# Third attention: scores as three F32R products, keys kept as high and low parts and replaced in place

## The chip, the cores and the metric

The program runs on one core of one Trainium2 chip, as one launch. The metric is the device time of an execution in microseconds; lower is better. Five engines work side by side, each with a queue of its own: TensorE (PE, with its weight loads as PEld), VectorE (DVE), ScalarE (ACT), GpSimd (POOL) and SyncE (SP), which here issues the DMAs. They wait for one another by semaphores.

## The reference

The input is x (64 batches of 128 rows of 128 numbers) and a context of 64 x 77 x 96. Eight layers follow one another, each adding to x: attention 0 (16 heads, masked), a SiLU layer, attention 1 (8 heads), a quantised layer, attention 2 (16 heads, this case), a gated mixture of experts, a wide attention and a routed mixture. Attention 2, which the text calls the third attention, computes

```
q = (x @ Wq).reshape(b, n, h, d).transpose(0, 2, 1, 3)      # h = 16 heads, d = 64; x is normalised first
k = (context @ Wk).reshape(b, -1, h, d).transpose(0, 2, 1, 3)
v = (context @ Wv).reshape(b, -1, h, d).transpose(0, 2, 1, 3)
sim = jnp.einsum('bhid,bhjd->bhij', q, k) * scale
attn = jax.nn.softmax(sim, axis=-1)
out = jnp.einsum('bhij,bhjd->bhid', attn, v)
return out.transpose(0, 2, 1, 3).reshape(b, n, h * d) @ Wo + bo
```

## The kernel before

Weights are folded first: with Wq Wk^T per head (mt) the scores are z times "keys", where keys = mt^T times the context (128 x 77 per head and batch) and z is the normalised x, turned; with Wv Wo per head (vo) the output is a sum over heads of probabilities times "values" (77 x 128 per head and batch). Projections of keys and values are made as three F32R products of high and low parts (`three_passes`, lines 84 to 89): high x high, low x high, high x low. The scores and the weighted sum are plain F32 matmuls.

The class `CrossAttention` is one program for three attentions. The batches run in order, t = 0 to 63; four make a group, eight a window (i = 0 to 7 within it, k = i mod 4). One batch has 16 x 77 = 1232 score columns in three PSUM banks (6, 6 and 4 heads: 462, 462 and 308 columns). `window` in `tensor` (974 to 1013) does for batch t: transposes of the probabilities of t (`turn_chunks`, ten blocks in three uses of ps_t), then the scores of batch t+2 (`scores`, line 891), at k = 1 the turning of the next group's z, then the weighted sum of batch t (`weighted_sum`, line 904). Between these, `project_next` sets projections, in the order of a plan written out by hand (lines 613, 614): keys of the next group, `key_plan` (4,3,2,5,4,5,2,7), and values of the next window, `val_plan` (3,4,4,2,3,2,2,0). One key projection is one head for four batches (308 columns), one value projection 128 or 104 rows by 512 columns; they use the two banks ps_p in turn. 32 keys and 20 values a window.

The keys stand in two buffers, one per group parity (line 650). ScalarE copies key projections there (`copy_keys`, 1022), value projections into one of five staging slots (`copy_values`, 1031), from which SyncE stores two projections at a time to HBM (`store_values`, 822); `load_values` (835, 837) fetches each batch's values two batches ahead. ScalarE also copies the transposed probabilities (1059, 1062) and z (1049), and takes the exponentials (1067) in the order of `window` in `scalar`: copies of t's transposes, then the exponentials of t+1, then the remaining projections' copies.

VectorE's order per batch (`body`, 1266): at k = 1 z of the next group (236); `normalise` of batch t+1 (reduce 1197, reciprocal 1199, multiply 1205); `shift` of batch t+2 (maxima 1153, subtractions 1189 from PSUM into the buffer e, two of which alternate); the residual of batch t (1221); statistics (190, 195, 290, 292). The subtractions free the score banks; the exponentials wait for them. GpSimd has small work: per group the bias (225), two powers (209, 304) and their sums, per window two copies that reorder the context (`copy_window`, 1390), for which it waits until the window's last probabilities are done (1342). Ahead of the loop stands a start-up: 20 values, 16 + 7 keys, z, the scores of batches 0 and 1.

## Time and profile before

| what | us |
|---|---|
| median of three runs | 2406.95 (2406.39 to 2409.49) |
| the profiled execution | 2405.5 |
| its span, first to last instruction | 2403.6 |
| TensorE busy | 2222.6 (92%) |
| VectorE busy | 1857.5 (77%) |
| ScalarE busy | 1492.9 (62%) |
| GpSimd busy | 685.1 (29%) |
| granted TensorE clock, mean | 0.961 of full speed |

The page's 40 slices are 60 us each. TensorE's digits are 9 nearly everywhere; the third attention fills slices 21 to 30 (about 1240 to 1840 us), where GpSimd's digit is mostly 1. A timeline row gives start, duration, engine, line, operation, written tile and read tiles, and "x3" means three merged instructions. Durations overlap on an engine, since instructions are pipelined; the pace is the distance of starts. A plain F32 matmul shows as two records.

### The profile page before, as it was taken

The numbers are of one execution on the slowest core, as the hardware profiler recorded it, in microseconds if no ns is written. First come the engines' busy times: TensorE is split into PE (matmuls) and PEld (weight loads), VectorE is DVE, ScalarE is ACT, GpSimd is POOL, SyncE is SP. The second block draws the span as 40 slices with busy tenths as digits, with TensorE's granted clock in tenths as the row PEclk, the third lists the DMA queues.
The fourth block names the chain that finished last, engine by engine and source line by source line (L and its number), as shares of the span: only waits on it lengthen the run. The fifth ranks groups of instructions, "written<-read, shape, count | busy, mean of one in ns | idle before, by whom it ended". The sixth has DMA issues, their size and how long they took to land.

```text
span 2403.6 us, 49297 instructions
## 1 busy us (share of the span) xinstructions
PE 2222.6 (92%) x14668; PEld 1910.2 (79%) x14669; DVE 1857.5 (77%) x4483; ACT 1492.9 (62%) x3090; POOL 685.1 (29%) x926
## 2 busy tenths in 40 slices
PE   7899999999899899995478999999997999979999
PEld 6688888888698788872257888888886888879998
DVE  3688888888976888887975887887888666866666
ACT  5566666665445677767886666666664654636666
POOL 2255546555412122210001111111102442422334
PEclk9999999999999999997589999999998999979999
DMA  8444554445201444430025445454442000114545
GB/s 216 114 137 129 145 144 138 134 140 151 68 0 47 114 133 126 137 111 15 0 72 146 132 134 153 137 145 140 140 132 62 1 1 3 37 53 139 141 140 158
DMA packets 461646, 256.58 MB, mean 107 GB/s; under 512 B 25664, under 2 KB 442332, under 8 KB 461532
## 3 DMA queue, kind: packets, MB, share of 16 engines
q1 hardware_dynamic: 461532, 255.27, 37.7%
q8 instruction: 46, 0.75, 0.1%
q14 instruction: 68, 0.56, 0.1%
HBM read 150.10 MB, written 105.12 MB: 106 GB/s over the span
## 4 chain that ended last, share of the span: by engine, by line
PE 75%; DVE 12%; ACT 6%; issue 5%; POOL 0%; ACTq 0%; DVEq 0%; POOLq 0%
PE ps_o L904 13%; PE ps_s L891 11%; PE ps_p L87 7%; PE ps_p L89 6%; PE ps_p L88 6%; PE ps_t L881 6%; PE ps_o L1474 3%; PE ps_t L1474 2%; PE ps_t L3129 2%; PE ps_s L3111 2%; PE ps_o L3129 2%; PE ps_s L87 2%; ACT a_keys L1022 2%; DVE a_sm L1197 2%; PE ps_s L89 2%
## 5 line engine op out<-in xcount | busy, mean ns | idle before, releaser
L904 PEld LDWEIGHTS ps_o<-a_val,a_pt 128*128 128x128 f32 (+2 forms) x3200 | 413.6, 192 | 35.0 <-issue 8.4
L904 PE MATMUL ps_o<-a_val,a_pt 128*128 128x128 f32 (+2 forms) x3200 | 423.9, 276 | 5.7 <-ACT a_pt L1059 3.6
L891 PE MATMUL ps_s<-a_keys,a_zt 128*128 128x308 f32 (+1 forms) x1024 | 415.7, 492 | 14.6 <-ACT a_keys L1022 9.8
L1031 ACT ACTIVATE a_stage<-ps_p 128x512 f32<-128x512 f32 (+1 forms) x370 | 221.1, 598 | 276.9 <-PE ps_p L89 275.0
L1197 DVE TENSOR_REDUCE a_sm<-a_e 128x16 f32<-128x1232 f32 (+1 forms) x192 | 234.2, 1220 | 183.2 <-ACT a_e L1067 182.7
L1059 ACT ACTIVATE a_pt<-ps_t 128x512 f32<-128x512 f32 (+1 forms) x448 | 225.2, 505 | 151.1 <-PE ps_t L881 149.8
L1022 ACT ACTIVATE a_keys<-ps_p 128x308 f32<-128x308 f32 x603 | 256.7, 427 | 81.8 <-PE ps_p L89 81.4
L881 PE MATMUL ps_t<-ident,a_e 128*128 128x128 f32 (+1 forms) x1600 | 262.8, 277 | 32.9 <-POOL a_e L1214 16.4
L87 PE MATMUL ps_p<-ct_hi,a_mt_hi 96*128 (+1 forms) x603 | 293.0, 486 | 0.0
L1067 ACT ACTIVATE a_e<-a_e 128x1232 f32<-128x1232 f32 (+1 forms) x192 | 203.9, 1062 | 50.9 <-DVE a_e L1189 34.6
L1214 POOL TENSOR_TENSOR a_e<-a_e,a_rs 128x539 f32<-128x539 f32 (+1 forms) x192 | 165.6, 890 | 234.6 <-DVE a_rs L1202 233.2
L881 PEld LDWEIGHTS ps_t<-ident,a_e 128*128 128x128 f32 (+1 forms) x1600 | 194.1, 140 | 44.0 <-issue 19.0
L87 PE MATMUL ps_p<-a_vo_hi,a_windowhi 96*128 96x512 f32 (+1 forms) x370 | 207.9, 562 | 5.2 <-ACT a_keys L1022 3.9
L891 PEld LDWEIGHTS ps_s<-a_keys,a_zt 128*128 128x128 f32 x1024 | 169.5, 191 | 41.5 <-issue 22.5
L89 PE MATMUL ps_p<-ct_hi,a_mt_lo 96*128 (+1 forms) x603 | 184.3, 306 | 0.0
L88 PE MATMUL ps_p<-ct_lo,a_mt_hi 96*128 (+1 forms) x603 | 184.0, 305 | 0.0
L1153 DVE TENSOR_REDUCE a_mx<-ps_s 128x6 f32<-128x462 f32 (+1 forms) x320 | 155.9, 533 | 27.2 <-PE ps_s L891 26.9
L225 POOL TENSOR_TENSOR x<-x,a_bias 128x512 f32<-128x512 f32 (+1 forms) x48 | 61.3, 1276 | 340.9 <-DVE z L353 203.4
L1189 DVE TENSOR_TENSOR a_e<-ps_s,a_mx 128x462 f32<-128x462 f32 (+1 forms) x320 | 154.3, 532 | 0.0
L1205 DVE TENSOR_TENSOR a_e<-a_e,a_rs 128x616 f32<-128x616 f32 (+1 forms) x128 | 146.2, 1142 | 4.4
L88 PEld LDWEIGHTS ps_p<-ct_lo,a_mt_hi 96*128 96x128 f32 x603 | 116.4, 193 | 39.0 <-issue 32.1
L89 PE MATMUL ps_p<-a_vo_hi,a_windowlo 96*128 96x512 f32 (+1 forms) x370 | 146.3, 395 | 0.0
(437 smaller groups left out, 4931.6 us busy)
## 6 DMA issues: line engine op xcount, KB each, us to landing
a_vals<-a_stage SPq DMA_DIRECT2D x160, 512.0 KB, 3.5
a_val<-a_vals SPq DMA_DIRECT2D x128, 576.0 KB
f_w<-in_L_ffn_W_dram SPq DMA_DIRECT2D x129, 256.0 KB, 2.7
a_vals<-a_stage SPq DMA_DIRECT2D x40, 416.0 KB
a_val<-a_vals SPq DMA_DIRECT2D x64, 256.0 KB
a_val<-a_vals SPq DMA_DIRECT2D x128, 40.0 KB
x<-in_x_dram SPq DMA_DIRECT2D x8, 512.0 KB, 7.0
out_dram<-x SPq DMA_DIRECT2D x7, 512.0 KB, 6.8
```

The costliest lines, as they stand in the source:

```text
L87: eng.matmul(out, lhs[0], rhs[0], start=start, stop=False)
L88: eng.matmul(out, lhs[0], rhs[1], start=False, stop=False)
L89: return eng.matmul(out, lhs[1], rhs[0], start=False, stop=stop)
L881: mm = eng.transpose(c.ps_t[0:w, slot, (i % GT) * P:(i % GT + 1) * P], src[:, P * i:P * i + w], c.ident[:, :])
L891: eng.matmul(c.ps_s[:, b, 0:nh * KEYS], zt, keys[:, h0:h0 + nh, :], start=True, stop=True)\
L904: mm = eng.matmul(c.ps_o[:, (i % 2) * P:(i % 2 + 1) * P], self.pt[0:r, n, :], self.val[0:r, i % 2, n, :], start=(n == 0), stop=(n == self. ...
L1022: eng.activation(self.keys[:, par, :, h, :], bank[:, 0:GCOLS].rearrange("p (b k) -> p b k", b=GT), ACT.Copy)\
L1031: eng.activation(self.stage[0:n, slot, BANK * (v % 2):BANK * (v % 2) + BANK], bank[0:n, :], ACT.Copy)\
L1059: mm = eng.activation(dst[:, i0:full, :], src[:, 0:full - i0, :], ACT.Copy)
L1067: eng.activation(self.e[:, par, :], self.e[:, par, :], ACT.Exp).then_inc(self.exp_ready.sem, 1)
L1197: eng.tensor_reduce(self.sm[:, :], e, AX.X, ALU.add).then_inc(st.sem, 1)
L1214: eng.tensor_tensor(e[:, heads, :], e[:, heads, :], bc(self.rs[:, par, heads], KEYS), ALU.mult)\
```

## The change

Only the third attention changes (`split=name == "L2"`).

- z and keys are held as F32R high and low parts. `scores` issues `three_passes` for each of the three banks, instead of one F32 matmul.
- z: ScalarE's copy now writes the high part; VectorE writes the low part (`split_zt`, one subtraction of 128x512 from PSUM), at k = 1 after `shift`.
- There is one keys buffer (a high and a low one) in place of two. `freed_by` gives for each scored batch the four heads of the next group that its space takes; the layout alternates between group parities (`unit_of`, `batch_of`). The plan has four keys a batch; each stands on TensorE after the scores that free its space: one behind the third bank, one behind the first and second part of the weighted sum, the last at its end. Values go 3,3,3,3,3,3,2,0, ahead of them.
- ScalarE copies a key projection into a ring of four slots (`keep_keys`), waiting until GpSimd has split what was there. GpSimd makes both parts (`split_keys`: a cast and a dependent subtraction of 128x308) and no longer waits for probabilities ahead of `copy_window`. At k = 2, TensorE waits before each bank of scores for the last split that this bank reads.
- Staging slots go from five to two; the first window's values also use e and pt for staging, so VectorE's first `shift` and ScalarE's loop wait for those stores.
- Start-up: 20 values and 16 keys, whose low parts VectorE writes (`split_first_keys`), then z and its low part, scores of batches 0 and 1, and only then eight keys of the next group, copied by ScalarE around its first exponentials and split by GpSimd. The next layer's weight split on GpSimd comes after them.

```diff
+        self.split, self.in_place = split, split and H == 16
+        self.slots = 2 if self.in_place else self.STAGES
+        self.first_rounds = self.units // self.STAGES
+        self.rounds = self.units // self.slots
         self.key_plan = (4, 3, 2, 5, 4, 5, 2, 7) if H == 16 else (2, 2, 1, 2, 2, 2, 2, 3)
         self.val_plan = (3, 4, 4, 2, 3, 2, 2, 0) if H == 16 else (2, 1, 2, 1, 2, 2, 0, 0)
+        if self.in_place:
+            self.val_plan = (3, 3, 3, 3, 3, 3, 2, 0)
...
-        self.first = self.vuses + H + self.key_plan[-1]
+        self.early_keys = 2 * self.quads if self.in_place else 0
+        self.lead = self.vuses + H + (0 if self.in_place else self.key_plan[-1])
+        self.first = self.lead + self.early_keys
...
-        self.keys = sb(ctx, n("keys"), [P, 2, GT, H, KEYS], F32)
+        if split:
+            self.keys_hi, self.keys_lo = (sb(ctx, n("keys" + h), [P, 1 if self.in_place else 2, GT * H, KEYS], F32R)
+                                          for h in ("hi", "lo"))
+            self.zt_lo = sb(ctx, n("ztlo"), [P, 2, GT * P], F32R)
+            self.unsplit = sb(ctx, n("unsplit"), [P, self.RING, GT, KEYS], F32)
+        else:
+            self.keys = sb(ctx, n("keys"), [P, 2, GT, H, KEYS], F32)
...
-        self.stage = sb(self.stage_scope, n("stage"), [P, self.STAGES, self.PART * P], F32)
+        self.stage = sb(self.stage_scope, n("stage"), [P, self.slots, self.PART * P], F32)
...
+    def freed_by(self, k, par):
+
+        q = self.quads
+        return [2 * k, 2 * k + 1, 2 * k + 8, 2 * k + 9] if par == 0 else [q * k + j for j in range(q)]
+
+    def make_plan_in_place(self, last):
+
+        plan, place, v = [], 0, 0
+        for i in range(self.WIN):
+            mine = []
+            if not last:
+                for _ in range(self.val_plan[i]):
+                    mine.append(("v", v, place))
+                    v, place = v + 1, place + 1
+            if not last or i < 2:
+                for h in self.freed_by((i + 2) % GT, self.key_group(i) % 2):
+                    mine.append(("k", h, place))
+                    place += 1
+            plan.append(mine)
...
+    def batch_of(self, keys, par, k, b):
+
+        h0, nh = self.head_span(b)
+        if not self.in_place:
+            return keys[:, par].rearrange("p (k h) c -> p k h c", k=GT)[:, k, h0:h0 + nh, :]
+        if par == 0:
+            return keys[:, 0].rearrange("p (k h) c -> p k h c", k=GT)[:, k, h0:h0 + nh, :]
+        pairs = keys[:, 0].rearrange("p (m k h) c -> p m k (h c)", k=GT, h=2)
+        return pairs[:, h0 // 2:(h0 + nh) // 2, k, :]
...
+    def stage_of(self, w, u):
+
+        if not self.in_place or not (isinstance(w, int) and w == 0):
+            return u % self.slots, u // self.slots, self.stage[:, u % self.slots, :]
+        slot, width = u % self.STAGES, self.PART * P
+        places = [self.stage[:, 0, :], self.stage[:, 1, :], self.e[:, 0, 0:width], self.e[:, 1, 0:width],
+                  self.pt[:, 0:width // P, :].rearrange("p i d -> p (i d)")]
+        return slot, u // self.STAGES, places[slot]
...
-    def scores(self, eng, t, b, zt, keys, first=False):
+    def scores(self, eng, t, b, par, k, first=False):
 
         c = self.core
         h0, nh = self.head_span(b)
         if not first:
             eng.wait_ge(self.scores_read.sem, self.scores_read.at(self.NB * (t - 1) + b + 1))
-        eng.matmul(c.ps_s[:, b, 0:nh * KEYS], zt, keys[:, h0:h0 + nh, :], start=True, stop=True)\
-           .then_inc(self.scores_ready.sem, 1)
+        o, cols = c.ps_s[:, b, 0:nh * KEYS], slice(k * P, k * P + P)
+        if self.split:
+            mm = three_passes(eng, o, [z[:, par, cols] for z in (self.zt_hi, self.zt_lo)],
+                              [self.batch_of(keys, par, k, b) for keys in (self.keys_hi, self.keys_lo)])
+        else:
+            mm = eng.matmul(o, self.zt[:, par, cols], self.keys[:, par, k, h0:h0 + nh, :], start=True, stop=True)
+        mm.then_inc(self.scores_ready.sem, 1)
...
+                if self.split and u - 5 >= self.vuses:
+                    eng.wait_ge(self.key_split.sem, self.key_split.at(u - 5 - self.vuses + 1))
...
+        for n in range(self.early_keys):
+            u = self.lead + n
+            if n >= 2:
+                eng.wait_ge(self.proj_copied.sem, self.proj_copied.at(u - 1))
+            self.project_keys(eng, c.ps_p[:, n % 2, :], 1, self.freed_by(n // self.quads, 1)[n % self.quads])
...
+                        if k == 2 and self.split:
+                            eng.wait_ge(self.key_split.sem,
+                                        self.key_split.at(self.keys_for(w, par, b, last) + 1))
+                        elif k == 2:
                             eng.wait_ge(self.proj_copied.sem,
                                         self.proj_copied.at(self.keys_use(w, par, b, last) + 1))
-                        self.scores(eng, t + 2, b, self.zt[:, par2, n2 * P:(n2 + 1) * P], self.keys[:, par2, n2])
-                        project_next()
+                        self.scores(eng, t + 2, b, par2, n2)
+                        project_next(scored=b == self.NB - 1)
...
+                    project_next(self.WIN if j == self.uses - 1 else 1, scored=True)
...
+    def keep_keys(self, eng, u, bank, n, slot):
+
+        eng.wait_ge(self.key_split.sem, self.key_split.at(n - self.RING + 1))
+        eng.wait_ge(self.proj_done.sem, self.proj_done.at(u + 1))
+        eng.activation(self.unsplit[:, slot, :, :], bank[:, 0:GCOLS].rearrange("p (b k) -> p b k", b=GT), ACT.Copy)\
+           .then_inc(self.proj_copied.sem, 1)
...
+        slot, turn, place = self.stage_of(w, unit)
         if v % 2 == 0 and not (isinstance(w, int) and w == 0 and turn == 0):
-            eng.wait_ge(self.stored[slot].sem, self.stored[slot].at(16 * (self.rounds * w + turn)))
+            eng.wait_ge(self.stored[slot].sem, self.stored[slot].at(self.stored_by(w, turn)))
...
+        for n in range(min(2, self.early_keys)):
+            self.keep_keys(eng, self.lead + n, c.ps_p[:, n % 2, :], self.heads + n, (self.heads + n) % self.RING)
         self.exponentials(eng, 0, 0)
+        for n in range(2, self.early_keys):
+            self.keep_keys(eng, self.lead + n, c.ps_p[:, n % 2, :], self.heads + n, (self.heads + n) % self.RING)
+        if self.in_place:
+            eng.wait_ge(self.stored[4].sem, self.stored[4].at(16 * self.first_rounds))
...
+    def split_first_keys(self, eng):
+
+        for u in range(self.vuses, self.lead):
+            g, h = (u - self.vuses) // self.heads, (u - self.vuses) % self.heads
+            eng.wait_ge(self.proj_copied.sem, self.proj_copied.at(u + 1))
+            bank = self.core.bank(u % 5)[:, 0:GCOLS].rearrange("p (b k) -> p b k", b=GT)
+            eng.tensor_tensor(self.unit_of(self.keys_lo, g % 2, h), bank,
+                              self.unit_of(self.keys_hi, g % 2, h).bitcast(F32), ALU.subtract)\
+               .then_inc(self.key_split.sem, 1)
+
+    def split_zt(self, eng, g, par, u, slot):
+
+        eng.wait_ge(self.t_copied.sem, self.t_copied.at(u + 1))
+        eng.tensor_tensor(self.zt_lo[:, par, :], self.core.ps_t[:, slot, :],
+                          self.zt_hi[:, par, :].bitcast(F32), ALU.subtract).then_inc(self.zt_split.sem, 1)
...
+                if self.split and k == 1 and not last:
+                    u = 1 + self.gcyc * g + 2 * self.uses
+                    self.split_zt(eng, g + 1, 1 - par, u, (1 + self.gcyc * par + 2 * self.uses) % 2)
...
-        if self.next_stats and not self.setup:
+        if self.next_stats and not self.setup and not self.split:
             self.after.split_weights(eng)
         v_last = max(place for mine in self.plan for kind, _, place in mine if kind == "v")
...
+    def split_keys(self, eng, u, n, par, h):
+
+        src = self.unsplit[:, n % self.RING, :, :]
+        hi, lo = self.unit_of(self.keys_hi, par, h), self.unit_of(self.keys_lo, par, h)
+        eng.wait_ge(self.proj_copied.sem, self.proj_copied.at(u + 1))
+        eng.tensor_copy(hi, src).then_inc(self.key_high.sem, 1)
+        eng.wait_ge(self.key_high.sem, self.key_high.at(n - (self.lead - self.vuses) + 1))
+        eng.tensor_tensor(lo, src, hi.bitcast(F32), ALU.subtract).then_inc(self.key_split.sem, 1)
+
+    def gpsimd_split(self, eng, v_last):
+
+        for n in range(self.early_keys):
+            self.split_keys(eng, self.lead + n, self.lead - self.vuses + n, 1,
+                            self.freed_by(n // self.quads, 1)[n % self.quads])
+        self.ln.pool(eng, 1)
+        if self.next_stats:
+            self.after.split_weights(eng)
+
+        def window(w, more, last):
+            for i in range(self.WIN):
+                for kind, h, place in self.plan_of(i, last):
+                    if kind == "k":
+                        self.split_keys(eng, self.use(w, place), self.key_number(w, place, last),
+                                        self.key_group(i) % 2, h)
+                g = 2 * w + 1 + i // GT
+                if last and i >= GT:
+                    break
+                if i % GT == 2:
+                    self.ln.pool_bias(eng, g)
+                    if self.left and g >= 3:
+                        self.left.root(eng, g - 3)
+                    if self.next_stats and g >= 2:
+                        self.next_stats.pool(eng, g - 2)
+                    if more and i >= GT:
+                        eng.wait_ge(self.proj_done.sem, self.proj_done.at(self.use(w, v_last) + 1))
+                        self.copy_window(eng, w + 2)
+                elif i % GT == 3 and g + 1 < GROUPS:
+                    self.ln.pool(eng, g + 1)
...
+            banks_free=(ahead.added, GROUPS - 1) if name == "L1" else None, split=name == "L2")
```

## Rows read from the trace of the kernel before

**Rows 1.** Stretch, length, busy us (instructions) by engine, clock, DMA share, GB/s

```profile
1410.83:1482.48 71.65, 71.65 (x454) 61.30 (x452) 57.82 (x121) 44.74 (x95) 9.79 (x13) 1.00 0.49 141
```

**Rows 2.** Chain of waits in the third attention: start us, us, what

```profile
1410.24 0.78 PE ps_s L891 x2
1411.45 0.52 PE ps_s L891 x2
...
1416.45 0.44 PE ps_t L881 x4
...
1421.87 2.23 PE ps_o L904 x20
```

**Rows 3.** Timeline of TensorE at that attention's first projections: start us, us, instruction

```profile
1264.87 0.39 PE L89 MATMUL ps_p<-a_vo_hi,a_windowlo 96*104 96x512 f32 x1
1265.10 0.30 PE L87 MATMUL ps_s<-ct_hi,a_mt_hi 96*128 96x308 f32 x1
1265.24 0.31 PE L88 MATMUL ps_s<-ct_lo,a_mt_hi 96*128 96x308 f32 x1
```

**Rows 4.** Timeline of VectorE and ScalarE over one batch, idle time before in brackets

```profile
1410.83 1.44 DVE L1197 TENSOR_REDUCE a_sm<-a_e 128x16 f32<-128x1232 f32 x1 [1.34 <-ACT a_e L1067]
...
1412.59 1.44 DVE L1205 TENSOR_TENSOR a_e<-a_e,a_rs 128x1232 f32<-128x1232 f32 x1
...
1413.94 1.56 DVE L1153 TENSOR_REDUCE a_mx<-ps_s 128x6 f32<-128x462 f32 x3
...
1415.42 1.56 DVE L1189 TENSOR_TENSOR a_e<-ps_s,a_mx 128x462 f32<-128x462 f32 x3
...
1418.90 1.24 ACT L1067 ACTIVATE a_e<-a_e 128x1232 f32<-128x1232 f32 x1
...
1420.17 1.44 DVE L1197 TENSOR_REDUCE a_sm<-a_e 128x16 f32<-128x1232 f32 x1 [2.58 <-ACT a_e L1067]
```

**Rows 5.** Timeline of VectorE in the last window

```profile
1802.24 1.43 DVE L1197 TENSOR_REDUCE a_sm<-a_e 128x16 f32<-128x1232 f32 x1
...
1809.71 1.44 DVE L1197 TENSOR_REDUCE a_sm<-a_e 128x16 f32<-128x1232 f32 x1 [0.16 <-ACT a_e L1067]
```

**Rows 6.** GpSimd's groups by shape, whole run: busy us, mean ns | idle before

```profile
L1214 POOL TENSOR_TENSOR a_e<-a_e,a_rs 128x539 f32<-128x539 f32 x128 | 136.7, 1089 | 234.6 <-DVE a_rs L1202 233.2
...
L1214 POOL TENSOR_TENSOR a_e<-a_e,a_rs 128x154 f32<-128x154 f32 x64 | 31.5, 492 | 0.0
...
L1390 POOL CAST a_windowlo<-ct_lo 96x616 fp32r x5 | 6.4, 1285 | 0.0
...
L2313 POOL TENSOR_TENSOR f_w1lo<-f_w,f_w1hi 128x576 fp32r<-128x576 f32 x1 | 1.4, 1442 | 0.1
...
L2311 POOL CAST f_w1hi<-f_w 128x576 fp32r<-128x576 f32 x1 | 0.7, 682 | 0.0
...
L2616 POOL TENSOR_TENSOR a_wklo<-a_wk,a_wkhi 96x128 fp32r<-96x128 f32 x1 | 0.5, 453 | 0.1
...
L2615 POOL CAST a_wkhi<-a_wk 96x128 fp32r<-96x128 f32 x1 | 0.3, 286 | 0.1
```

**Rows 7.** Durations of two VectorE lines, ns min/median/max

```profile
L1205 DVE TENSOR_TENSOR a_e<-a_e,a_rs x59: 799/800/1149, 800.8 to 1079.4; 128x616 f32<-128x616 f32 x59
...
L3222 DVE TENSOR_SCALAR f_z<-x,tail_mean_var,tail_rstd x64: 333/339/1325, 2138.4 to 2375.0; 128x128 f32 x48, 128x128 f32<-128x128 f32 x16
```

**Rows 8.** Timeline of GpSimd and VectorE where both work

```profile
152.88 1.67 POOL L1390 CAST a_windowlo<-ct_lo 96x616 fp32r<-96x616 f32 x1
...
877.17 1.28 POOL L225 TENSOR_TENSOR x<-x,a_bias 128x512 f32 x1 [9.68 <-DVE z L353]
...
877.96 1.15 DVE L1205 TENSOR_TENSOR a_e<-a_e,a_rs 128x616 f32<-128x616 f32 x1
```

**Rows 9.** Stores of values (line 822), from 1300 to 1800 us

```profile
DMA to landing us min/median/max: 3.2/3.5/5.2
```

**Rows 10.** Timeline of TensorE at that attention's first transposes, idle in brackets

```profile
1287.16 1.11 PE L881 MATMUL ps_t<-ident,a_e 128*128 128x128 f32 x4 [5.27 <-DVE a_e L1205]
```

More of the change, by code:

```diff
@@ L588 @@
     BLOCKS = -(-KEYS // KBLOCK)
+    RING = 4
     STAGES = 5
@@ L1094, in scalar @@
         eng.wait_ge(self.prod_done.sem, self.prod_done.at(self.pairs))
-        for u in range(self.first):
+        for u in range(self.lead):
             if u < self.vuses:
```

130 lines of the change are left out of this document (100 added, 30 removed).

## The prediction

> **What bounds the kernel now.** I read the page's slices first, then one window of eight batches of the third attention, then its chain of waits, then each engine's timeline inside it. That attention runs from about 1240 to 1840 us; its loop repeats windows of 71.65 us, in which TensorE is busy all 71.65, VectorE 57.82, ScalarE 44.74 and GpSimd 9.79 [rows 1]. TensorE bounds it, at full granted clock. The reader should see in the chain that a score bank of 462 columns costs 0.78 us, one of 308 0.52, four transposes 0.44, the ten blocks of the weighted sum 2.23 [rows 2]. F32R passes follow each other after 0.23 us at 512 columns (1264.87 to 1265.10) and after 0.14 at 308 [rows 3], so a value projection is 3 x 0.23 = 0.69 and a key projection 0.42. Ten transposes are 2.5 times four, 1.10; turning z is four more. Check: 8 x (1.10 transposes + 2.08 scores + 2.23 sum) + 32 keys x 0.42 + 20 values x 0.69 + 2 x 0.44 for z = 71.4, against 71.65.
>
> Behind TensorE stands a ring: exponentials, VectorE's normalise (reduce, reciprocal, multiply: 3.11 from 1410.83 to 1413.94), maxima 1.48, subtractions 1.48, then exponentials again 1.24 [rows 4]. It needs about 7.4 us a batch, and in the last window, where TensorE has almost nothing to project, batches follow at 7.47 [rows 5]. On average TensorE takes 8.96, so the ring has about 1.5 us to spare; the multiply of 1412.59 ends at 1414.03 and TensorE wants it at 1416.45 [rows 2, 4].
>
> **The change part by part.** *Scores.* A pass of 462 columns lies between 0.14 and 0.23; by interpolation 0.21, so 0.62 for three against 0.78; the small bank takes 0.42 against 0.52. Saved: 2 x 0.16 + 0.10 = 0.42 us a batch, 3.4 a window. Ends: if the pass costs what 512 columns do, 0.28 a batch; at 0.20, 0.46.
>
> *Plan.* Values go 3,3,3,3,3,3,2,0 and keys four a batch, the same 20 and 32 in all. TensorE's batches become 4.99 (1.10 + 1.66 + 2.23) + 1.68 keys + 2.07 values = 8.74, 9.18 where z is turned, 8.05 in batch 6, and 6.67 in batch 7. Batch 7 is then shorter than the ring's 7.47, with some wait on a port (below) 7.7: 1.0 lost a window. Before, seven keys stood there (4.99 + 0.42 + 7 x 0.42 = 8.35).
>
> *z in two parts.* VectorE adds one PSUM-SBUF subtraction of 512 columns every four batches, some 0.55 us; it comes after the subtractions, where the next normalise waits for the exponentials anyway (idle 2.58 us before 1420.17 in [rows 4]). Costs nothing in the loop; 0.55 at the start.
>
> *Keys in two parts.* ScalarE's copy is the same size, now into a ring of four slots. GpSimd gets a cast and a subtraction of 128x308 per head, four a batch. The rows nearest: the cast is 0.286 at 128 columns and 0.682 at 576, by interpolation 0.445 at 308; the subtraction 0.453 and 1.442, so 0.85 [rows 6]. With about 0.07 between the dependent pair: 1.36 us a head. Lower end: the attention's own GpSimd multiply, 1.089 at 539 and 0.492 at 154 columns, gives 0.73 at 308, with the cast 1.2. Upper end: if writing chunks of 77 hurts a cast as the window copy's scattered reads hurt it (1.285 at 616 columns, so 0.64) and the subtraction rises alike to 1.05, 1.75. I take 1.36 because the form of those rows (F32R out, two full F32 inputs) is the same. Per window: 32 x 1.36 = 43.5, plus the 9.8 of today = 53.3.
>
> *The port.* VectorE's multiply of probabilities in the second attention takes 0.80 alone, and 1.15 where GpSimd's addition of 877.17 was still running as it began: it ended 0.66 after that addition. In the other direction GpSimd's cast of 152.88 took 1.67 for 1.285, beside a VectorE operation on two SBUF inputs. VectorE's scaling of z takes 0.339, and up to 1.325 beside GpSimd's work [rows 6 to 8]. So multiply and GpSimd exclude each other, and each waits for the other's running instruction; reductions and operations that read PSUM show no such stretch. The Trainium skill has this as a rule ("SBUF — State Buffer", section "SBUF: two separate sides"): an operation with two SBUF inputs and a GpSimd operation hold a shared pair of ports whole; the trace agrees. A multiply of 1.44 a batch blocks GpSimd up to 11.5 a window, eight z operations of 0.26 another 2.1. GpSimd's window: 53.3 + 13.6 = 66.9, of TensorE's 68.25 plus losses. It fits, barely, but not evenly. VectorE in turn waits some 0.3 for GpSimd before a multiply; its slack of over 1 us covers that in batches with three values, not in batch 7 (the 7.7 above).
>
> *The new wait.* The scores of batches 2 and 6 read a new group of keys, so TensorE waits for GpSimd's last splits; everything in TensorE's queue (scores, values, sums) stands behind that, and VectorE's maxima wait for it. From the last key projection to the third bank of the next batch are 1.10 + 3 x 0.69 + 2 x 0.62 = 4.4 us. After a quiet stretch GpSimd gets the first of four keys 5.7 us into the batch, is held by the multiply to about 7.5 and ends the fourth 3.2 to 3.7 into the next batch: in time by 0.7 or more. After batch 6 it is not quiet: bias and statistics (2.6) and the window copies (2.5) come on top, no longer held back by their wait for the probabilities. Followed on, GpSimd ends the keys of batch 7 about 9.1 us into batch 0, those of batch 0 9.2 into batch 1, those of batch 1 5.3 into batch 2: 0.9 late, once a window. With 1.43 a head it is 2.3.
>
> *Stores.* Two staging slots instead of five: ScalarE waits for a store two units back, issued at least 8.3 us earlier; stores land in 3.2 to 5.2 us [rows 9]. Nothing, with 3 us to spare; if that cover went, ScalarE and both projection banks would stand.
>
> *Start.* Seven keys fewer ahead of the first scores, 7 x 0.42 = 2.9 gained; 0.55 for z's low part; 0.35 for GpSimd's early splits meeting the first multiplies: 2.0 gained. The eight early keys go into the 5.27 us in which TensorE waits for probabilities today [rows 10]. Shift's wait for the stores from the e buffer: they had landed by then. Last window: ring-bound before and after, 0.
>
> Sum: a window 71.65 - 3.4 + 1.0 + 0.9 = 70.15, 1.5 gained, seven times 10.5, and 2.0 at the start: 12.5 us. The profiled execution took 2405.5 (span 2403.6), so 2393.0; the median of the three runs is 1.45 above it, 2406.95, so **2394.5**.
>
> **The rivals.** *GpSimd short by a little* (1.43 to 1.5 a head): 2.3 or more late a window, gain 0.1 or less: 2401 to 2407, take 2405. For it: 66.9 of 68 is no margin. Against: interpolated prices. Chance 0.16.
>
> *GpSimd becomes the bound.* Place: the splits, 32 heads a window. At p us a head its window is 32p + 9.8 + 13.6, with some 1.5 of idling; it passes 71.65 from p = 1.46 on if every lock falls due, from 1.55 if some don't, and the wait shows as TensorE standing in batches 2 and 6 and ScalarE standing at its ring. At 1.6: 76.1, less the locks that don't fall due (about 3): 73, slower by 1.5 x 7 - 2 = 8.5: 2415; at 1.75: 78, 2449. For: chunks of 77, no row has that shape. Chance 0.20, at 2416.
>
> *The port matters little.* If multiplies and splits seldom meet, GpSimd has 53.3 of work and is never late: 71.65 - 3.4 + 0.9 = 69.15, so 7 x 2.5 + 2 = 19.5: 2387.5. With batch 7 not losing either: 2381. Against: the first split arrives at 5.8, the multiply at 6.0, in nearly each batch. Chance 0.18.
>
> *The passes are no faster*, because each needs its own weight load and that sets the pace: 1.0 + 0.9 lost a window, 7 x 1.9 - 2 = 11.3: 2418. Against: at 308 columns passes with a load each follow in 0.14 [rows 3]. Chance 0.04.
>
> **How the numbers follow.** Forecast 0.42 (2388 to 2400), the others as above. No change means within 0.2%, about what a measurement of this kernel can tell: 2402 to 2412. Faster: 0.42 + 0.18 + 0.03 = 0.63. Within: 0.13 of the first rival and 0.02 of the second = 0.15. Slower: 0.22. The range reaches from the rival at 2382 to the bound at 2418, leaving 0.07 below and 0.12 above.
>
> **What would show it.** Right: score banks in the chain at 0.62 and 0.42; windows near 70.2; GpSimd busy 52 to 55 a window with casts near 0.45 and subtractions near 0.85 unless a multiply lies on them; multiplies stretched from 1.44 to 1.6 to 1.9; batch 7 at 7.7; a TensorE wait for GpSimd's key parts of about 1 us in batch 2. Wrong: subtractions above 1 us, TensorE waiting for key parts in each group, ScalarE waiting for the ring or a store, or the ring of softmax pacing all batches.

## The result, and the profile after

The changed kernel is slower: 2421.56 us (2419.98 to 2427.11) against 2409.49 (2406.39 to 2411.1) for the kernel before on the same chip, a ratio of 1.0057 with a 95% interval of 1.0046 to 1.0069. The forecast was 2394.5 and faster. The profiled execution took 2421.56 us, its span 2419.8; the one before took 2405.5 and 2403.6.

The first look is at the same stretch as [rows 1]: eight batches of the third attention, from one normalise (L1345, first operation on VectorE) to the ninth. Columns: stretch, length, busy us (instructions) of TensorE, its weight loads, VectorE, ScalarE and GpSimd, granted clock, DMA share, GB/s.

```profile
1416.24:1489.69 73.45, 69.95 (x478) 64.02 (x477) 60.29 (x122) 46.84 (x95) 56.46 (x76) 1.00 0.48 137
```

The window has grown from 71.65 to 73.45 us. TensorE has less to do (69.95 for 71.65) and for the first time it waits. Seven windows of 1.8 us are 12.6 of the 15.8 us by which the attention, from its first value projection to its last residual, is longer (593.4 before, 609.3 after). The steps that shorten TensorE's work are there: this is TensorE's timeline, the passes of one score bank of 462 columns.

```profile
1278.05 0.38 PE L88 MATMUL ps_s<-a_keyslo,a_zthi 128*128 128x462 f32 x1
1278.26 0.37 PE L89 MATMUL ps_s<-a_keyshi,a_ztlo 128*128 128x462 f32 x1
1278.47 0.37 PE L87 MATMUL ps_s<-a_keyshi,a_zthi 128*128 128x462 f32 x1
```

They follow each other after 0.21 us, so three are 0.63 where one F32 product was 0.78 [rows 2]. What took the gain back is in TensorE's waits over the whole run (us in total, times, longest):

```profile
PE ps_t L985 <- DVE a_ztlo L1385: 14.2, 15, 2.1
PE ps_p L87 <- POOL a_windowlo L1614: 8.4, 6, 1.4
```

Neither is the wait that the prediction had costed (scores for GpSimd's key parts); that one doesn't occur in the whole run. The first, in the timelines of VectorE, ScalarE and TensorE:

```profile
1454.54 1.44 DVE L1353 TENSOR_TENSOR a_e<-a_e,a_rs 128x1232 f32<-128x1232 f32 x1
1455.90 1.56 DVE L1301 TENSOR_REDUCE a_mx<-ps_s 128x6 f32<-128x462 f32 x3
1457.38 1.56 DVE L1337 TENSOR_TENSOR a_e<-ps_s,a_mx 128x462 f32<-128x462 f32 x3
1458.86 0.68 DVE L1385 TENSOR_TENSOR a_ztlo<-ps_t,a_zthi 128x512 fp32r<-128x512 f32 x1
```
```profile
1454.19 0.60 ACT L1187 ACTIVATE a_zthi<-ps_t 128x512 fp32r<-128x512 f32 x1
```
```profile
1457.52 0.60 PE L985 MATMUL ps_t<-ident,a_e 128*128 128x128 f32 x4
...
1459.67 0.54 PE L985 MATMUL ps_t<-ident,a_e 128*128 128x128 f32 x3 [0.85 <-DVE a_ztlo L1385]
```

Turned z lies in one of the two slots of `ps_t`. ScalarE has written its high part by 1454.79, but VectorE reads the slot again for the low part, only after the maxima and subtractions, at 1458.86. The second transposes of the next batch need that slot and stand until 1459.67. It happens once a group, twice a window.

The second, in the timelines of GpSimd and TensorE:

```profile
1433.60 1.28 POOL L225 TENSOR_TENSOR x<-x,a_bias 128x512 f32<-128x512 f32 x1
1434.85 0.19 POOL L297 TENSOR_TENSOR tail_var<-tail_mean_var,eps 128x4 f32<-128x4 f32 x1
1435.12 1.02 POOL L304 TENSOR_TENSOR tail_rstd<-tail_var,neg_half 128x4 f32<-128x4 f32 x1
1436.20 2.34 POOL L1614 CAST a_windowhi<-ct_hi 96x616 fp32r<-96x616 f32 x1
1438.50 1.22 POOL L1614 CAST a_windowlo<-ct_lo 96x616 fp32r<-96x616 f32 x1
```
```profile
1439.77 0.50 PE L87 MATMUL ps_p<-a_vo_hi,a_windowhi 96*128 96x512 f32 x1 [1.41 <-POOL a_windowlo L1614]
```

The context of the next window is copied by GpSimd behind eight splits, the bias and the statistics, and batch 0 of that window projects its first value from it: 1.41 us, once a window. Batches are counted from 0 to 7 here, as in the prediction.

### The profile page after: what moved, and what is told of

It reads as the page before. It is cut to its first block, busy times and chain, and to the rows that moved or that the text cites. A ratio compares the mean times of both kernels' runs of the same rounds, so it can differ in the third digit from the quotient of the medians.

```text
span 2419.8 us, 50496 instructions
## 1 busy us (share of the span) xinstructions
PE 2211.7 (91%) x14860; PEld 1934.1 (80%) x14861; DVE 1886.0 (78%) x4515; ACT 1509.5 (62%) x3090; POOL 1033.6 (43%) x1406
## 4 chain that ended last, share of the span: by engine, by line
PE 66%; DVE 16%; ACT 7%; issue 5%; POOL 3%; ACTq 0%; DVEq 0%; POOLq 0%
PE ps_o L1013 10%; PE ps_p L87 6%; PE ps_s L1000 6%; PE ps_p L89 5%; PE ps_p L88 5%; PE ps_t L985 5%; PE ps_o L1698 3%; DVE a_sm L1345 3%; PE ps_s L87 3%; PE ps_t L1698 2%; PE ps_t L3353 2%; PE ps_s L89 2%; PE ps_s L88 2%; PE ps_o L3353 2%; PE ps_s L3335 2%
## 5 line engine op out<-in xcount | busy, mean ns | idle before, releaser
L1013 PE MATMUL ps_o<-a_val,a_pt 128*128 128x128 f32 (+2 forms) x3200 | 429.3, 276 | 5.7 <-ACT a_pt L1197 3.6
L1345 DVE TENSOR_REDUCE a_sm<-a_e 128x16 f32<-128x1232 f32 (+1 forms) x192 | 234.2, 1220 | 179.1 <-ACT a_e L1205 178.8
L87 PE MATMUL ps_p<-ct_hi,a_mt_hi 96*128 (+1 forms) x608 | 264.7, 435 | 2.3 <-ACT a_unsplit L1149 2.2
L1000 PE MATMUL ps_s<-a_keys,a_zt 128*128 128x308 f32 (+1 forms) x640 | 252.9, 481 | 12.8 <-ACT a_keys L1158 9.8
L1568 POOL TENSOR_TENSOR a_keyslo<-a_unsplit,a_keyshi 128x308 fp32r<-128x308 f32 x240 | 229.4, 956 | 19.2
L87 PE MATMUL ps_p<-a_vo_hi,a_windowhi 96*128 96x512 f32 (+1 forms) x370 | 191.4, 517 | 13.7 <-POOL a_windowlo L1614 8.4
L1149 ACT ACTIVATE a_unsplit<-ps_p 128x308 f32<-128x308 f32 x240 | 102.5, 427 | 162.2 <-PE ps_p L89 158.8
L1158 ACT ACTIVATE a_keys<-ps_p 128x308 f32<-128x308 f32 x362 | 153.8, 427 | 43.7 <-PE ps_p L89 43.3
L1566 POOL CAST a_keyshi<-a_unsplit 128x308 fp32r<-128x308 f32 x240 | 123.4, 514 | 113.8 <-ACT a_unsplit L1149 113.2
```

The source lines that it names most:

```text
L87: eng.matmul(out, lhs[0], rhs[0], start=start, stop=False)
L1000: mm = eng.matmul(o, self.zt[:, par, cols], self.keys[:, par, k, h0:h0 + nh, :], start=True, stop=True)
L1013: mm = eng.matmul(c.ps_o[:, (i % 2) * P:(i % 2 + 1) * P], self.pt[0:r, n, :], self.val[0:r, i % 2, n, :], start=(n == 0), stop=(n == self. ...
L1345: eng.tensor_reduce(self.sm[:, :], e, AX.X, ALU.add).then_inc(st.sem, 1)
L1568: eng.tensor_tensor(lo, src, hi.bitcast(F32), ALU.subtract).then_inc(self.key_split.sem, 1)
```

## The experiments

Theory A: these two waits alone turn the prediction's gain into a loss, and the rest of its sum holds. Rival B: the round of VectorE and ScalarE (the prediction's ring: exponentials, normalise, maxima, subtractions), or GpSimd, or the port it shares with VectorE, is the true limit, and the waits are where it happens to show. Ratios below are to the kernel before, run on the same chip; a percentage between two changed kernels is the difference of their ratios.

### Each wait alone, and both

```diff
-                if not (last and k >= 2):
-                    self.shift(eng, t + 2, k % 2, found)
                 if self.split and k == 1 and not last:
                     u = 1 + self.gcyc * g + 2 * self.uses
                     self.split_zt(eng, g + 1, 1 - par, u, (1 + self.gcyc * par + 2 * self.uses) % 2)
+                if not (last and k >= 2):
+                    self.shift(eng, t + 2, k % 2, found)
```

> The changed kernel with one step moved on VectorE: in the second batch of a group it forms the low part of the turned z right after the multiply, ahead of the maxima and subtractions of the batch after next. Theory A (TensorE's second transposes of every third batch wait 0.85 us for that low part, 12.1 us in 14 places, and nothing else is late there): those waits go, the window of eight batches falls from 73.45 to about 71.7 us, and the kernel by about 12 us, from 2421.6 to about 2409.5. Rival B (the round of VectorE and ScalarE, made longer by the stretched multiplies, is as late as TensorE; the wait is only where it shows): the subtractions come 0.7 us later, TensorE waits for the probabilities instead, and the kernel stays within 3 us of 2421.6.

Measured: ratio 0.9993 (0.9983 to 1.0003), 0.64% under the changed kernel, 15 us. The window is 71.26, 2.19 less; 7 x 2.19 = 15.3. In VectorE's timeline of this kernel the low part now stands straight behind the multiply, ahead of the maxima, and TensorE's second transposes start without a wait.

```profile
1449.70 1.44 DVE L1353 TENSOR_TENSOR a_e<-a_e,a_rs 128x1232 f32<-128x1232 f32 x1
1451.06 0.68 DVE L1385 TENSOR_TENSOR a_ztlo<-ps_t,a_zthi 128x512 fp32r<-128x512 f32 x1
1451.66 0.63 DVE L1301 TENSOR_REDUCE a_mx<-ps_s 128x6 f32<-128x462 f32 x1
```

The wait cost 1.1 us each time, not the 0.85 printed: the end of a TensorE record is modelled and reaches into the idle time. The window copy:

```diff
             for i in range(self.WIN):
+                if more and i == 6:
+                    eng.wait_ge(self.proj_done.sem, self.proj_done.at(self.use(w, v_last) + 1))
+                    self.copy_window(eng, w + 2)
                 for kind, h, place in self.plan_of(i, last):
...
-                    if more and i >= GT:
-                        eng.wait_ge(self.proj_done.sem, self.proj_done.at(self.use(w, v_last) + 1))
-                        self.copy_window(eng, w + 2)
```

> The changed kernel with one step moved on GpSimd: the copy of the next window's context (two casts, 4.1 us at the mean) stands ahead of the seventh batch's key splits instead of behind them, the bias and the statistics; GpSimd had 3.50 us idle there. Theory A (TensorE's first value projection of a window waits 1.41 us for that copy, six times): that wait goes, the window falls by about 1.4 us, the kernel by about 8.5 us to about 2413. Rival B (the key splits, now up to 1 us later, fill the ring of four, and ScalarE and then TensorE wait for them in batches 7 and 8 instead): the window stays within 0.5 us, the kernel within 3 us of 2421.6.

Measured: ratio 1.0026 (1.0014 to 1.0038), 0.31% or 7.5 us under the changed kernel. The window is 71.84, 1.61 less; six times that is 9.7, a little more than the kernel's time shows. Both moves together:

> Both moves together (low part of z ahead of the maxima on VectorE; window copy ahead of the seventh batch's splits on GpSimd). Theory A (TensorE is the bound and these two waits are all that the change added to its queue in a window): window 73.45 - 1.7 - 1.4 = about 70.35 us, near TensorE's busy 69.95; kernel 2421.6 - 12 - 8.5 = about 2401, faster than the kernel before (2409.5) by about 0.35%. Rival B (another engine holds the round at about 72 us): the two gains don't add, and the kernel stays above 2408.

Measured: 2395.09 us (2392.28 to 2397.07), ratio 0.9951 (0.9937 to 0.9965), which is 1.06% or 25 us under the changed kernel. The stretches of the three, one from each:

```profile
1429.38:1500.64 71.26, 69.47 (x478) 64.09 (x477) 60.27 (x122) 46.64 (x94) 56.45 (x77) 1.00 0.50 142
```
```profile
1436.22:1508.06 71.84, 69.74 (x478) 64.01 (x477) 60.03 (x122) 46.80 (x94) 56.59 (x77) 1.00 0.49 141
```
```profile
1427.34:1497.07 69.73, 69.30 (x478) 64.17 (x477) 60.05 (x122) 46.58 (x94) 56.53 (x77) 1.00 0.51 145
```

The gains add: 2.19 + 1.61 = 3.80, against 73.45 - 69.73 = 3.72, and in the kernel 7 x 2.19 + 6 x 1.61 = 25.0. VectorE, ScalarE and GpSimd are as busy as ahead of the moves. Rival B falls for these two waits.

### The start

```diff
+        self.exponentials(eng, 0, 0)
         for n in range(min(2, self.early_keys)):
             self.keep_keys(eng, self.lead + n, c.ps_p[:, n % 2, :], self.heads + n, (self.heads + n) % self.RING)
-        self.exponentials(eng, 0, 0)
```

> As the one with both moves, and ScalarE takes the first batch's exponentials ahead of the two early key copies. Theory: the first multiply comes 1.9 us earlier (the exponentials then start when VectorE's first subtractions end, 1281.8 for 1285.6), and the kernel is about 2 us under the one with both moves, about 2399. Rival: the second batch's exponentials stand behind the same key copies and GpSimd's ring anyway, so that the first batches end where they did and nothing is gained.

Measured: 2389.93 us (2388.01 to 2393.41), ratio 0.9938 (0.9925 to 0.9952), 0.13% or 3 us under the one without this edit, inside the intervals of the two. The first two normalises, of the changed kernel and of this one (VectorE's timelines):

```profile
1286.84 1.44 DVE L1345 TENSOR_REDUCE a_sm<-a_e 128x16 f32<-128x1232 f32 x1 [1.84 <-ACT a_e L1205]
1296.99 1.44 DVE L1345 TENSOR_REDUCE a_sm<-a_e 128x16 f32<-128x1232 f32 x1 [6.82 <-ACT a_e L1205]
```
```profile
1281.40 1.43 DVE L1345 TENSOR_REDUCE a_sm<-a_e 128x16 f32<-128x1232 f32 x1
1290.47 1.44 DVE L1345 TENSOR_REDUCE a_sm<-a_e 128x16 f32<-128x1232 f32 x1 [5.84 <-ACT a_e L1205]
```

Counted from the attention's first value projection (1252.91 and 1249.36), the first comes at 33.93 and 32.04 us, the second at 44.08 and 41.11. VectorE no longer stands 1.84 for the exponentials, as expected. Part of the difference at the second is clock, as the stretch from 1288 to 1300 shows (the changed kernel, then this one; the clock is the figure after GpSimd's, and this one had 1.00 over the ten us before too): a mean of 0.72 is time at both levels, 1.2 and 2.4 GHz, 1.00 all at 2.4.

```profile
1288.00:1300.00 12.00, 12.00 (x60) 10.35 (x59) 5.04 (x6) 6.85 (x14) 11.38 (x16) 0.72 0.15 45
```
```profile
1288.00:1300.00 12.00, 12.00 (x81) 11.09 (x79) 9.23 (x15) 8.86 (x19) 11.22 (x18) 1.00 0.48 141
```

With all three edits the attention takes 579.5 us, 13.9 less than in the kernel before (593.4), and 7 x (71.65 - 69.69) = 13.7 of that are the windows.

### What the terms of the sum are worth

The next three start from the kernel with all three edits (window 69.69 us, its row below). First its scores as one F32 product of the high parts:

```diff
-            mm = three_passes(eng, o, [z[:, par, cols] for z in (self.zt_hi, self.zt_lo)],
-                              [self.batch_of(keys, par, k, b) for keys in (self.keys_hi, self.keys_lo)])
+            mm = eng.matmul(o, self.zt_hi[:, par, cols].bitcast(F32),
+                            self.batch_of(self.keys_hi, par, k, b).bitcast(F32), start=True, stop=True)
```

> The kernel with both moves and the early exponentials, with the scores as one F32 product of the high parts: it leaves out the low parts, all splits are still made. This puts back the scores' price of the kernel before (0.78 + 0.78 + 0.52 = 2.08 us a batch for 1.68) and nothing else. Theory A: 8 x 0.42 = 3.4 us more a window, 69.7 -> 73.1, the kernel about 25 us slower, 2415. Rival (the gain of the three passes is partly lost at their seams, a pass after another kind of product starting late): under 2.5 more a window, under 18 us.

Measured: 2416.03 us, ratio 1.0029 (1.0017 to 1.0042), 0.91% or 22 us above the kernel with three passes; 7 x 3.03 = 21.2. The window is 72.72:

```profile
1421.45:1491.14 69.69, 69.30 (x478) 64.13 (x477) 60.01 (x122) 46.63 (x94) 56.49 (x77) 1.00 0.51 145
```
```profile
1428.39:1501.11 72.72, 72.33 (x454) 60.77 (x452) 60.82 (x123) 46.61 (x94) 57.15 (x77) 1.00 0.48 139
```

The passes save 3.03 a window, between the two expectations and a little nearer to 3.4. It also prices all the rest of the change, once the two waits are gone: 72.72 - 71.65 = 1.07 a window. The prediction had 1.0 for the plan. One thing more differs between the two kernels, VectorE's multiply in batch 6 (with three passes, then with one F32 product):

```profile
1485.30 1.59 DVE L1353 TENSOR_TENSOR a_e<-a_e,a_rs 128x1232 f32<-128x1232 f32 x1
```
```profile
1494.88 1.98 DVE L1353 TENSOR_TENSOR a_e<-a_e,a_rs 128x1232 f32<-128x1232 f32 x1
```

It is 1.98 in every window of the F32 kernel, where GpSimd's subtraction of 1494.78 was still running as it began, and the first scores of batch 7 wait for VectorE's work behind it (they begin 1.87 us after the batch's first transposes, where the kernel with a value moved, below, needs 1.48). So up to 0.4 of the 3.03, and of the 1.07, may be the port and not the passes or the plan: an estimate from these two rows, which no run separates. Then with one F32R product instead of three:

```diff
+            mm = eng.matmul(o, self.zt_hi[:, par, cols], self.batch_of(self.keys_hi, par, k, b),
+                            start=True, stop=True)
```

> The kernel with both moves and the early exponentials, with one F32R product for the scores instead of three: it leaves out both products with low parts, the splits are all still made. TensorE has 8 x 2 x (0.21 + 0.21 + 0.14) = 9.0 us less a window. Theory A (TensorE alone sets 69.7 us): the window falls to where VectorE (busy 60.0) and its ring take over, 61 to 64 us, the kernel by 40 to 60 us from 2390. Rival (the ring of VectorE, ScalarE and the shared port is nearly as long as TensorE's 69.7): the window stays above 67, the kernel falls by under 20 us.

Measured: 2368.24 us, ratio 0.9833 (0.9818 to 0.9848), 1.05% or 25 us less.

```profile
1420.41:1486.31 65.90, 62.99 (x431) 55.92 (x430) 60.47 (x122) 45.62 (x95) 55.75 (x77) 1.00 0.54 153
```

By the pitches TensorE lost 9.0 us of work a window, and the window 3.8. Neither expectation held: the next limit is at 65.9, above the 61 to 64 of A and under the 67 of B. TensorE's waits there are nearly all for VectorE (its multiply 1.2 us, its z 1.0, its subtractions 0.2), so this limit is the round, with VectorE's multiplies stretched beside GpSimd from 8 x 1.44 by 1.4 us in all. So TensorE leads by only 3.8 us a window, and single short batches may already go at the round's pace; batch 7 below does in part. Without GpSimd's subtractions:

```diff
-        eng.tensor_copy(hi, src).then_inc(self.key_high.sem, 1)
-        eng.wait_ge(self.key_high.sem, self.key_high.at(n - (self.lead - self.vuses) + 1))
-        eng.tensor_tensor(lo, src, hi.bitcast(F32), ALU.subtract).then_inc(self.key_split.sem, 1)
+        eng.tensor_copy(hi, src).then_inc(self.key_split.sem, 1)
```

> The kernel with both moves and the early exponentials, without GpSimd's subtractions: the low parts of all keys after the first group's are left out (stale values stand there), the casts stay. GpSimd's busy time falls from 56.5 to about 25 us a window. Theory A (GpSimd and the port it shares with VectorE are off TensorE's path in the steady window): the window stays at 69.7 within 0.3, the kernel within 4 us of 2390, the last four batches and the start included. Rival (stretched multiplies and late splits cost TensorE time): the window falls by over 0.7, the kernel by over 6 us.

Measured: 2390.34 us, ratio 0.9931 (0.9916 to 0.9946), the same within the intervals. GpSimd's busy time halves (27.25 for 56.49), the window is 69.54 for 69.69. The groups of VectorE that share the port, with subtractions and then without (busy, mean ns | idle):

```profile
L1353 DVE TENSOR_TENSOR a_e<-a_e,a_rs 128x1232 f32<-128x1232 f32 x8 | 11.8, 1473 | 0.3
L236 DVE TENSOR_SCALAR z<-x,ln_mean_var,ln_rstd 128x128 f32<-128x128 f32 x8 | 3.1, 451 | 0.0
```
```profile
L1353 DVE TENSOR_TENSOR a_e<-a_e,a_rs 128x1232 f32<-128x1232 f32 x8 | 11.6, 1456 | 0.3
L236 DVE TENSOR_SCALAR z<-x,ln_mean_var,ln_rstd 128x128 f32<-128x128 f32 x8 | 2.2, 335 | 0.0
```

z's scaling is back from 451 to 335 ns without any gain. The 0.15 has another place: the multiply in batch 6 takes 1.44 in every window, where it took about 1.6, and the first scores of batch 7 begin 1.72 us after its first transposes for 1.90. That is 1 us in the whole kernel, too little to see in its times. GpSimd's 29 us of subtractions a window cost no more than this as long as TensorE sets the pace.

### The plan

The even plan alone, in the kernel before:

```diff
+        if H == 16 and not self.masked:
+            self.key_plan = (4, 4, 4, 4, 4, 4, 4, 4)
+            self.val_plan = (3, 3, 3, 3, 3, 3, 2, 0)
```

> The kernel before, scores still one F32 product, with the changed kernel's plan alone in the third attention: four keys a batch, values 3,3,3,3,3,3,2,0. Theory A (the plan costs only what the seventh interval of a window loses, because it becomes shorter than the ring of softmax, 7.47 to 7.64 us): batch 7 has 4.99 + 0.42 + 4 x 0.42 = 7.09 us of TensorE's work, so 0.4 to 0.5 lost a window, window 71.65 -> about 72.1, kernel about 3 us above the kernel before (ratio about 1.001). Rival (the plan is what made the change slower, by moving values and keys into batches where TensorE then waits): window above 73, ratio 1.004 or more.

Measured: ratio 1.0055 (1.0041 to 1.0069), window 73.57. This looks like the rival of the expectation, and is as large as the loss of the change itself. Its timeline has a wait that neither the kernel before nor the changed one has inside a window: the last of the four keys of batch 2 (and of batch 6) is read by the scores of the same batch, where only two keys stood before.

```profile
1459.51 0.52 PE L894 MATMUL ps_s<-a_keys,a_zt 128*128 128x308 f32 x1 [0.59 <-ACT a_keys L1025]
```

Two of these a window are 1.2 us as printed. The plan that avoids them (keys 5,5,2,5,5,4,2,4, the same values, batch 7 with four keys for seven all the same) tells whether they were all:

> The kernel before with keys 5,5,2,5,5,4,2,4 and values 3,3,3,3,3,3,2,0 in the third attention: as the one with the plan alone, batch 7 has four keys for seven, but batch 2 keeps its two keys and batch 6 its two, so that no scores read a key projected in their own batch more than before. Theory A (the plan-alone kernel lost 1.2 us a window to TensorE's waits for ScalarE's copies of such keys, and the rest to the short batch 7): the waits go and 0.5 to 0.7 us a window stays, window 72.2 to 72.4, kernel 4 to 5 us above the kernel before (ratio 1.002). Rival (an even plan is dear by itself, by seams between F32 and F32R products): 73.5 again, ratio 1.005.

Measured: ratio 1.0 (0.9991 to 1.0009).

```profile
1428.28:1500.11 71.83, 71.83 (x454) 61.12 (x452) 57.64 (x121) 44.22 (x95) 9.81 (x12) 1.00 0.49 141
```

Without these waits 1.74 a window comes back, so they were nearly the whole loss (0.87 each, for 0.59 printed); the short batch 7 costs 0.2 here, less than the 0.5 expected. TensorE's batch 7 lasts 7.23 in it, less than the round's 7.47. So most of the 1.07 of the in-place version has to be looked for in its own batch 7, which lasts 7.59 for 6.67 of work. TensorE there, in the kernel with both moves:

```profile
1492.99 1.04 PE L985 MATMUL ps_t<-ident,a_e 128*128 128x128 f32 x8
1494.28 0.44 PE L985 MATMUL ps_t<-ident,a_e 128*128 128x128 f32 x2 [0.25 <-ACT a_pt L1197]
1494.89 0.47 PE L87 MATMUL ps_s<-a_keyshi,a_zthi 128*128 128x462 f32 x1 [0.18 <-DVE a_e L1337]
```

Ten transposes are 1.10 us by the price of [rows 2], and the first score pass starts 1.90 after the first of them: 0.8 lost, of which the records show 0.43 as waits. In this layout no key is projected between the transposes any more, because its space is free only after the scores; so the waits for ScalarE's copy and for VectorE's subtraction lie bare. Two ways to shift work, on the kernel with all three edits. A key from batch 6 to batch 7:

```diff
-                for h in self.freed_by((i + 2) % GT, self.key_group(i) % 2):
+                heads = self.freed_by((i + 2) % GT, self.key_group(i) % 2)
+                if i == 6:
+                    heads, late = heads[:-1], heads[-1:]
+                elif i == 7:
+                    heads = late + heads
+                for h in heads:
```

> The kernel with both moves and the early exponentials, and one key projection moved from batch 6 to batch 7 (batches counted from 0: three keys and five for four and four). Theory A (batch 7 is shorter than the round of softmax, so part of its time is lost, the prediction's 1.0 us): batch 6 falls from 8.18 to about 7.7 and batch 7 stays at 7.64; the window falls by 0.4 to 0.5 us, 69.7 -> 69.25, the kernel by 3 us, 2390 -> 2387. Rival (the loss isn't in batch 7: TensorE's records show only 0.4 us idle in the whole window): batch 7 grows by what batch 6 loses, 0.42, and nothing changes.

Measured: ratio 0.9945 (0.9932 to 0.9959), window 70.17: 0.5 longer. Both expectations were wrong. The key stands behind the scores, after the time that batch 7 loses. By the starts of TensorE's batches, batch 7 grows from 7.59 to 8.16 and batch 6 gives back only 0.16, because it already ended nearly with the round. In the kernel with both moves TensorE began batch 7 at 1492.99, 0.18 after this multiply ended:

```profile
1491.19 1.62 DVE L1353 TENSOR_TENSOR a_e<-a_e,a_rs 128x1232 f32<-128x1232 f32 x1
```

From this comes theory C: a value in batch 6, taken from batch 5, lets the round run ahead. Values 3,3,3,3,3,2,3,0:

> The kernel with both moves and the early exponentials, and one value projection moved from batch 5 to batch 6 (batches from 0: values 3,3,3,3,3,2,3,0). The key moved from batch 6 to batch 7 lost 0.46 us a window. Theory C, formed on it: batch 6 already ends with the round of softmax (TensorE begins batch 7 0.18 us after the multiply), and batch 7's transposes and first scores then stand for ScalarE's copy and VectorE's subtraction, since no key may be projected between them; 0.69 us of projection taken from batch 5, where the round has 1.9 us to spare, and put into batch 6 lets the round get ahead by that much and fills the time lost: the window falls by 0.5 to 0.7 us, 69.7 -> 69.1, the kernel by 3.5 to 5 us, to about 2386. Rival (TensorE's total work alone counts, nothing is lost in batch 7 that a later start could fill): window 69.7, kernel unchanged.

> As the one before, and another value moved from batch 4 to batch 6 (values 3,3,3,3,2,2,4,0). Theory C: at most what is left of the 1.0 us that batch 7 loses, so 0.1 to 0.4 us a window more, kernel 2384 to 2386. Rival (batches 4 and 5, now shorter, come to the round themselves, or the window copy on GpSimd, which waits for the last value, makes the key splits late): the window rises again by 0.3 or more.

Measured: 2388.86 us (2386.04 to 2392.03), ratio 0.9918 (0.9905 to 0.9932), and with the second value 2391.44, ratio 0.9922 (0.9909 to 0.9936). The windows:

```profile
1426.49:1495.78 69.29, 69.04 (x478) 64.13 (x477) 60.43 (x122) 46.56 (x94) 56.06 (x77) 1.00 0.50 146
```
```profile
1425.24:1494.72 69.48, 69.23 (x478) 64.07 (x477) 60.86 (x122) 46.59 (x94) 55.67 (x78) 1.00 0.50 146
```

0.4 of the lost time comes back, under the 0.5 to 0.7 expected: the first scores of batch 7 begin 1.48 us after its first transposes for 1.90, with no wait for VectorE. The second value gives nothing more. The first of the two has the lowest ratio of all kernels here that leave nothing out, 0.82% under the kernel before; its interval overlaps that of the one with the three edits alone (0.9925 to 0.9952), so in the kernel's time the gain is not clear of noise.

## Why the prediction was wrong, point by point

*What bounds the kernel:* right. TensorE sets the window before, and after it once it doesn't wait (69.30 busy of 69.73).

*Scores:* the mechanism was right, the size a little high: 3.03 a window for 3.4, and perhaps up to 0.4 less for the port (above). The pitches are as interpolated, 0.21 and 0.14, but for one: behind the transposes the first pass of a batch takes 0.30 to 0.32. Each batch gives 0.34 to 0.42, so the missing 0.4 is spread over the window; whether it is this first pass wasn't tried.

*Plan:* near in size, 1.07 (or up to 0.4 less) for 1.0, and half right in its reason. Batch 7 loses 0.8 ahead of its scores. Half of it is the round, as predicted: the wait for VectorE's subtraction, which goes when a value moved to batch 6 lets the round run ahead. The other half is the wait for ScalarE's copy of the transposes with nothing to do between them, and the prediction didn't have it. In the kernel before with a short batch 7 keys stand there and 0.2 is lost; but that batch also has 0.42 more work in its scores and no splits beside it, so the missing filler is argued from TensorE's timeline and not isolated by a run.

*z in two parts:* the step that failed. "It comes after the subtractions, where the next normalise waits for the exponentials anyway. Costs nothing in the loop" looks only at VectorE's own idle time. The subtraction is also the last reader of a `ps_t` slot, so its place in VectorE's queue sets when TensorE may go on. VectorE's idle time came after it, which helps nobody who waits for it. 2.19 a window, 15.3 us. TensorE's wait for `zt_split` stands in the changed code and its price could have been read before: in [rows 4] the subtractions end at 1416.90, so the low part would end at 1417.5, and TensorE wanted its second transposes one group of transposes (0.44) and a value (0.69) after 1416.45 [rows 2], near 1417.6. That is for a batch in which z isn't scaled. For batch 1, where it is, the timelines of VectorE and TensorE in the kernel before show the margin:

```profile
1450.01 1.56 DVE L1189 TENSOR_TENSOR a_e<-ps_s,a_mx 128x462 f32<-128x462 f32 x3
```
```profile
1452.30 0.60 PE L881 MATMUL ps_t<-ident,a_e 128*128 128x128 f32 x4
```

The subtractions end at 1451.5 and the low part would at 1452.1, 0.2 ahead of the second transposes of batch 2. Between batches 5 and 6 it would have come 0.3 late already (1489.15 for 1488.83), and the change makes TensorE's batches shorter.

*Keys in two parts:* prices good, 0.44 and 0.79 for 0.445 and 0.85, GpSimd 56.5 us a window for the predicted 53.3. *The port:* the lock is there (a multiply of 1.44 became 1.62 in the window, z's scalings 451 ns for 335), and it costs 0.15 a window, as the kernel without subtractions shows: only the multiply in batch 6 has TensorE waiting behind it. The rule of the Trainium skill that the prediction weighed ("SBUF — State Buffer", section "SBUF: two separate sides"), by which VectorE or GpSimd holds the shared ports for a whole instruction and the other waits, describes these stretches. Whether one matters depends on who waits for the stretched operation. The rivals that made GpSimd the bound fell.

*The new wait:* 0.9 was charged to scores waiting for GpSimd's keys; it didn't occur. The prediction followed GpSimd's queue through bias, statistics and window copies, and asked only when the key splits behind them would be ready, not when the copies themselves would be. The first value projection needs them 0.4 us into batch 0: 1.61 a window, 9.7 us by the windows. This is a second failed step, and the nearer one: the queue had been written out, with the late item in it.

*Stores:* right, no wait.

*Start:* 2.0 gained was predicted; the changed kernel has lost 2.5 by the fourth normalise (63.25 for 60.70 us from the first value projection), 1.1 of it by the first wait above. Ahead of its first scores TensorE stands 1.6 for z's low part, where it stood 0.7 for ScalarE's copy before: 0.9 for the 0.55 expected. The prediction had said that the eight early keys go into idle time, which is so for TensorE, but ScalarE copies two of them ahead of its first exponentials. With these first, the fourth comes at 58.88, 1.8 gained; in the kernel with the two moves alone it came at 63.10. These comparisons mix in the granted clock, which differed between executions in the first 50 us (0.93 over the projections of the changed kernel, 1.00 over those of the kernel before), so the size of this term is not settled.

*The sum:* 71.65 - 3.03 + 1.07 = 69.69 is the window with both waits gone (by construction, since both terms come from the same F32 run); 69.69 + 2.19 + 1.61 = 73.49 is the changed kernel's, measured 73.45. Without the two waits the kernel is at 0.9951 of the kernel before, where the prediction's 12.5 us are 0.9948. That they are so close is partly luck: its 70.15 holds a wait of 0.9 that never occurred and 0.4 more for the passes than they gave, and the 2.0 of the start weren't there.

## What to carry to other kernels

When a change inserts an operation, list who waits for it, not only what idle time its own engine has. An operation that reads a PSUM slot another engine will reuse belongs ahead of the long work on its queue, even if its result isn't needed for long: moving one 0.68 us subtraction ahead of 3 us of maxima and subtractions was worth 15 us here. When work is put into an engine's queue, check every other item of that queue for its own reader. And a slot in the order that can hold filler, as between two transposes that wait for a copy, seems worth something by itself: the in-place layout gave it up, for some 0.4 us a window by TensorE's timeline.

## What the runs showed of the hardware

- With three F32R passes for one F32 product the window fell by less than the pitches say (3.03 for 3.4). The first pass behind the transposes took 0.30 to 0.32 us for 0.21.
- Taking 29 us of GpSimd work out of a 69.7 us window moved the window by 0.15, the stretch of the one multiply that TensorE waited behind.
- TensorE's busy time hid part of its idle time. The printed wait of 0.85 was 1.1 in the window; of the 0.8 lost in batch 7 0.43 was printed. The Trainium skill ("Perfetto Trace Analysis", section "Tensor Engine Instruction (MATMUL, LD_WEIGHTS)") says that the profiler estimates TensorE's end times. The starts, and the pitches between them, are what to count by.
- GpSimd took 0.44 us for a cast and 0.79 for a two-input subtraction of 128x308 into chunks of 77 columns, no more than the prediction's interpolation from contiguous rows (0.445 and 0.85); a multiply lying on them made them 1.6 and 1.9.
